# Scale and shift of the first norm: a VectorE product and a GpSimd sum replaced by sixteen ScalarE activations per chunk

## The reference

```python
emb = jax.nn.silu(_sin_emb(timestep)) @ W_ada + b_ada
scale, shift = jnp.split(emb[:, None, :], 2, axis=-1)
x = _ln(src) * (1.0 + scale) + shift
q = (x @ Wq + bq)...            # k and v likewise, from the same x
...
x = x + (ctx @ Wo + bo)
```

## Time and profile before

| | before |
|---|---|
| median of 3 runs | 761.92 us (759.7 to 762.53) |
| profiled execution | 761.58 us, of which the span from first to last instruction is 759.8 us |
| mean granted TensorE clock | 0.857 |
| TensorE matmul busy | 577.8 us (76% of the span) |
| VectorE busy | 481.5 us (63%) |
| ScalarE busy | 262.7 us (35%) |
| GpSimd busy | 281.6 us (37%) |

### The profile page before, as it was taken

The page is one execution under the profiler, slowest core; times in us unless marked ns, Lnnn a source line. Parts: engine busy times, 40 slices in busy tenths (PEclk is TensorE's granted clock), DMA queues, the critical chain, the costliest instruction groups (busy, mean ns, idle before and its releaser), DMA issues.

```text
span 759.8 us, 16208 instructions
## 1 busy us (share of the span) xinstructions
PE 577.8 (76%) x5068; PEld 433.1 (57%) x5069; DVE 481.5 (63%) x1306; ACT 262.7 (35%) x548; POOL 281.6 (37%) x200
## 2 busy tenths in 40 slices
PE   3528678995969978589384871439999999999992
PEld 1415375583754747438383361327777787777771
DVE  5674784899679996717966127714656565655661
ACT  1215534524344153243231401004444444444440
POOL 0831628077055480564705010300423333323332
PEclk9558599998888999779785795559999999999997
DMA  8622474133064321553205673256223222222220
GB/s 291 234 78 66 145 251 141 34 112 110 2 227 190 102 82 40 177 239 112 102 9 166 230 278 137 97 192 227 44 40 47 44 42 42 44 41 36 49 42 1
DMA packets 41144, 86.28 MB, mean 114 GB/s; under 512 B 7317, under 2 KB 31790, under 8 KB 37006
## 3 DMA queue, kind: packets, MB, share of 16 engines
q1 hardware_dynamic: 22896, 65.13, 24.5%
q0 software_dynamic: 7200, 8.60, 6.6%
q10 hardware_dynamic: 11006, 12.01, 5.3%
HBM read 57.18 MB, written 29.44 MB: 114 GB/s over the span
## 4 chain that ended last, share of the span: by engine, by line
PE 55%; DVE 21%; DMA 8%; issue 5%; ACT 3%; POOL 3%; ACTq 3%; POOLq 0%; SPq 0%; DVEq 0%
PE bank L1563 8%; PE bank L1732 7%; PE bank L1554 6%; PE bank L1721 4%; PE bank L1723 4%; PE bank L1722 4%; DMA out_x<-x_kept,ids 4%; DMA stage<-in_moe_w 4%; PE bank L1733 3%; PE bank L1451 2%; PE bank L1518 2%; PE bank L1534 2%; PE bank L1508 2%; DVE split L914 2%; PE bank L1490 2%
## 5 line engine op out<-in xcount | busy, mean ns | idle before, releaser
L1721 PE MATMUL bank<-xs_f,w_moe 128*128 128x128 f16 x624 | 124.1, 221 | 6.9 <-issue 5.5
L1723 PE MATMUL bank<-xs_f,w_moe 128*128 128x128 f16 x624 | 124.1, 221 | 0.0
L1722 PE MATMUL bank<-xs_f,w_moe 128*128 128x128 f16 x624 | 123.6, 221 | 0.0
L825 ACT ACTIVATE stage<-bank,cols 128x128 f32<-128x128 f32 x312 | 88.5, 377 | 95.9 <-PE bank L1723 83.2
L629 POOL DMA_INDIRECT out_x<-x_kept,ids x39 | 61.9, 1587 | 65.0 <-DVE x_kept L1371 34.9
L1721 PEld LDWEIGHTS bank<-xs_f,w_moe 128*128 x624 | 61.4, 98 | 43.1 <-issue 14.1
L1732 PE MATMUL bank<-w_moe,split 128*128 x208 | 78.7, 380 | 0.7
L573 POOL DMA_INDIRECT dispatched<-disp,slot x32 | 34.1, 1067 | 121.0 <-DVE disp L1160 56.7
L1554 PE MATMUL bank<-w_moe 128*128 128x512 f32 x128 | 63.1, 656 | 16.2 <-ACT w_moe L707 16.2
L1416 PE MATMUL bank<-mats,w_moe 128*128 128x128 f32 x96 | 19.9, 375 | 57.2 <-DVE w_moe L957 57.2
L1722 PEld LDWEIGHTS bank<-xs_f,w_moe 128*128 x624 | 61.6, 99 | 2.6
(11 more groups left out here) (242 smaller groups left out, 1275.2 us busy)
## 6 DMA issues: line engine op xcount, KB each, us to landing
stage<-in_moe_w SPq DMA_DIRECT2D x16, 1024.0 KB, 7.8
w_split<-split SPq DMA_DIRECT2D x16, 1024.0 KB, 5.0
w_moe<-w_split SPq DMA_DIRECT2D x8, 2048.0 KB, 8.2
w_moe<-in_bias SPq DMA_DIRECT2D x8, 1024.0 KB, 11.0
xs<-dispatched ACTq DMA_DIRECT2D x41, 130.0 KB, 2.1
w_moe<-in_x_f SPq DMA_DIRECT2D x4, 512.0 KB, 5.6
w_moe<-in_x_t SPq DMA_DIRECT2D x4, 512.0 KB, 5.1
out_x<-x4b ACTq DMA_DIRECT2D x4, 512.0 KB, 5.4
```

Of the source, the lines that this page charges most:

```text
L825: ins = act.activation(h32[j][:, f, :], bank[2 * j + g][:, P * (f % 4):P * (f % 4) + P], ACT.Relu, bias=moe_b1[:, bass.ds(e, 1), f], scale ...
L1721: pe.matmul(o, hi, xs_f[j][:, k, :], start=(k == 0), stop=False)
L1722: pe.matmul(o, hi, xs_f[j][:, KD + k, :], start=False, stop=False)
L1723: mm = pe.matmul(o, lo, xs_f[j][:, k, :], start=False, stop=(k == KD - 1))
```

## The change

The product on VectorE and the sum on GpSimd are removed. ScalarE does both in one: for each feature half k and each of the 8 sequences b, one activation over 64 columns reads PSUM, multiplies with the scale and adds the shift of that sequence (both are one number per partition), and writes `x1`. That makes 16 activations per chunk. In ScalarE's order they stand: for chunk 0 ahead of `split_high(0, 0)`; for chunk 1 between `context(0, 1)` and `split_high(0, 3)`; for chunks 2 and 3 behind the feed-forward activations and ahead of `split_high(c + 1, 0)` and the exponentials.

```diff
-            def shift_norm(c):
-                for k in range(KD):
-                    pool.wait_ge(ada_scaled.sem, ada_scaled.of(c, k + 1))
-                    pool.tensor_tensor(
...
-                        ALU.add).then_inc(x1_ready.sem, 1)
...
             mask(0)
-            pool.wait_ge(cond_ready, 1)
-            shift_norm(0)
             select(1)
             less_maximum(0, 0)
             less_maximum(0, 1)
             probabilities(0, 0)
             probabilities(0, 1)
-            shift_norm(1)
             pool.wait_ge(main_in, N_MAIN)
             select(2)
             for c in range(NCH - 1):
...
                 less_maximum(c + 1, 0)
-                if c + 2 < NCH:
-                    shift_norm(c + 2)
                 less_maximum(c + 1, 1)
...
+            def scale_shift(c):
+                act.wait_ge(v_done.sem, v_done.of(c, 0))
+                act.wait_ge(kept_ready.sem, kept_ready.of(c, 0))
+                for k in range(KD):
+                    act.wait_ge(turn1_done.sem, turn1_done.of(c, k + 1))
+                    for b in range(CB):
+                        at = c * CB + b
+                        ins = act.activation(x1[:, k, S * b:S * b + S], bank[TURN1_BANK[c] + k][:, S * b:S * b + S],
+                                             ACT.Identity, bias=ada[:, KD + k, at:at + 1], scale=ada[:, k, at:at + 1])
+                    ins.then_inc(x1_ready.sem, 1)
...
+            act.wait_ge(cond_ready, 1)
+            scale_shift(0)
             act.wait_ge(main_in, N_MAIN)
             split_high(0, 0)
...
             context(0, 1)
+            scale_shift(1)
             split_high(0, 3)
...
                 feed_forward(c, range(KF))
+                if c + 2 < NCH:
+                    scale_shift(c + 2)
                 split_high(c + 1, 0)
                 exponentials(c + 1, 0)
...
-                def scale_norm():
...
-                        dve.tensor_tensor(x1[:, k, :].rearrange("p (b s) -> p b s", s=S),
...
-                                          ALU.mult).then_inc(ada_scaled.sem, 1)
...
             norms()
-            scale_norm()
             dve.wait_ge(main_in, N_MAIN)
...
             residual()
-            scale_norm, *_ = attention(1)
-            scale_norm()
             split_low(0, 3)
...
                 scores(0)
-                if c + 2 < NCH:
-                    scale_norm, *_ = attention(c + 2)
-                    scale_norm()
                 split_low(c + 1, 0)
```

More of the change, by code:

```diff
@@ L318, in build @@
         xn1_ready, turn1_done = count("xn1_ready", 1), count("turn1_done", 2)
-        ada_scaled, x1_ready = count("ada_scaled", 2), count("x1_ready", 2)
+        x1_ready = count("x1_ready", 2)
         q_done, q_ready = count("q_done", 2), count("q_ready", 2)
@@ L520, in mask @@
                             ALU.add).then_inc(bias_masked[u].sem, 1)
-            def shift_norm(c):
-                for k in range(KD):
-                    pool.wait_ge(ada_scaled.sem, ada_scaled.of(c, k + 1))
-                    pool.tensor_tensor(
-                        x1[:, k, :].rearrange("p (b s) -> p b s", s=S),
-                        x1[:, k, :].rearrange("p (b s) -> p b s", s=S),
-                        ada[:, KD + k, bass.ds(c * CB, CB)].unsqueeze(2).broadcast_to([P, CB, S]),
-                        ALU.add).then_inc(x1_ready.sem, 1)
             def less_maximum(c, u):
@@ L1000, in attention @@
                 vec, finish = stepper(attention_step, c)
-                def scale_norm():
[L1004 to L1007, removed]
-                        dve.tensor_tensor(x1[:, k, :].rearrange("p (b s) -> p b s", s=S),
-                                          bank[TURN1_BANK[c] + k][:].rearrange("p (b s) -> p b s", s=S),
-                                          ada[:, k, bass.ds(c * CB, CB)].unsqueeze(2).broadcast_to([P, CB, S]),
-                                          ALU.mult).then_inc(ada_scaled.sem, 1)
                 def values():
@@ L1037, in sums @@
                         finish()
-                return scale_norm, values, scores, sums
+                return values, scores, sums
             def second_half(c):
@@ L1181, in _ @@
             hidden, residual, norms = adapter(0)
-            scale_norm, values, scores, sums = attention(0)
+            values, scores, sums = attention(0)
             step(dve.tensor_copy(time_f[:], time_i[:]))
@@ L1269, in _ @@
             for c in range(NCH - 1):
-                _, values, scores, sums = attention(c + 1)
+                values, scores, sums = attention(c + 1)
                 (_, _, rotate, norm3, style, choose, token_gates, find_place, copy_gates, accumulate,
```

## The result

The changed kernel takes 763.98 us (median; 762.05 to 765.56), the kernel before 761.34 us on the same chips (759.44 to 762.64). The ratio is 1.0037, with a 95% interval of 1.0027 to 1.0047: it is slower by 2.1 to 3.6 us, 0.37%. The profiled execution is 764.33 us with a span of 762.5 us, against 761.58 and 759.8.

A forecast was written before the change was run, and what follows sets the result against it. The chain through TensorE (55% of the span) and VectorE (21%) was taken as the bound. 2.55 + 0.2 + 0.45 = +3.2 us on the profiled 761.58 gave 764.8; the median's 0.34 made 765.1 us, range 761.5 to 768.5.

The forecast's parts named there:

- The activations: ScalarE's sixteen 64-column activations per chunk: 0.404 us for one, 0.304 us from one to the next, 4.96 us in all.
- Rival (a): ScalarE's activations run slower than worked out, step 0.33 us or more: 766.5 us, up to 769.7; chance 0.25.
- The step itself: First norm, TensorE's transposes to queries: 0 in chunk 0; in chunk 1 queries at 116.19 against 116.09.
- The first selection: GpSimd's selection for chunk 1 moves forward into chunk 0's norm and stalls three VectorE operations: +2.55 us.
- Rival (b): The moved selections don't stall VectorE; chunk 0 costs 0 and chunk 1 0.1: 762.5 us; chance 0.15.
- The second selection: GpSimd's selection for chunk 2 moves into chunk 1's norm; 2.4 us of cover, 0.1 to 0.15 us comes through.
- The cover behind chunk 1's norm: VectorE's 9.49 us idle ahead of 131.29 covers split_low(0, 3) and norm2 ending some 3.5 us later: cost 0.
- Turn c = 0: Loop, chunk 2: split_low ends later, so GpSimd's probabilities start and VectorE's rotation step ends 0.45 us later: +0.45 us.
- Turn c = 1: Loop, chunk 3: the same sequence, but the part split ends before less_maximum lets VectorE in: cost 0.
- (c): Loop, chunk 2: VectorE's rotation slips in ahead of GpSimd's probabilities and wins up to 1.9 us; chance 0.07.
- (d): ScalarE reloads its table for the new activations, 1.3 us, twice in the loop, hitting waiting time; chance 0.01.

The follow-up runs named there:

- the two with shared norm: On the kernel with both repairs, ScalarE does the first feature half and VectorE the second, in chunks 0 and 1 (753.29 us) or chunk 1 alone (754.89 us).
- the filler: The kernel before, with 32 unread transposes on TensorE between chunk 1's transposes and its queries: 761.21 us, ratio 0.9996.
- the moved rotation: The kernel before, with the rotation's odd half ahead of the first half's probabilities on GpSimd: 758.19 us against 762.15, ratio 0.9958.

## Why the prediction was right

The sign, the size and both places were right: 765.1 us forecast, 763.98 measured. By its steps:

- **The activations.** Forecast 4.96 us, measured 4.83 or 4.84 in the three chunks shown. Both terms were off and partly cancel: one takes 439 ns and not 404, and the step from one to the next is (4.84 - 0.44) / 15 = 0.293 us and not 0.304. The first error lies in the price of a column. The two lengths that the prediction names, 1.91 us at 2048 columns and 775 ns at 512, give 0.74 ns and not 0.83, and with 0.74 ns the 775 ns come down to 444 ns at 64 columns. The second is the overlap, 0.439 - 0.293 = 0.146 us, where the rows at 512 columns gave 0.10. So a total within 0.12 us is partly luck. Rival (a), whose step was 0.33 us or more, is out. By the Trainium skill, "ScalarE: Activation LUTs", section "What ACT_TABLE_LOAD costs", one would take 0.425 us and, with an overlap of 93 ns, the sixteen 5.4 us, both estimates. The trace agrees on the one and not on the overlap, and so not on the sixteen.
- **The step itself.** Forecast 0 and, by the shorter transposes of chunk 1, +0.1 us; measured -0.1 us in both chunks, since the sixteen are 0.12 us shorter than worked out.
- **The first selection.** Forecast +2.55 us from a collision that stood elsewhere in the trace; measured +2.54. The edit that holds the selections takes the loss away, and the edit that moves them alone brings all of it. Rival (b) is out. (The +2.54 is this pair of traces; over all thirteen it is 2.3 to 2.8 us.)
- **The second selection.** Forecast +0.1 us through the cover of 2.4 us; nothing came through. The norm ends at 112.56 + 1.38 = 113.94, and TensorE transposes at 114.47 with no idle time ahead. Holding this selection alone gave no gain that can be told.
- **The cover behind chunk 1's norm.** Forecast as cost 0 with 9.49 us idle on VectorE. The idle time ahead of the same operation (now L970) is 6.29 us: 3.2 us of it went, where 3.5 were forecast:

```profile
135.43 0.68 DVE L970 TENSOR_TENSOR w_moe<-bank,add_o 64x512 f32<-64x512 f32 x1 [6.29 <-PE bank L1416]
```

- **Turn c = 0.** Forecast +0.45 us, measured 20.67 - 20.19 = +0.48 us, and L1061 longer by 0.50 us.
- **Turn c = 1.** Forecast 0, and this step failed. L1061 grew by 0.80 us. It takes two things together. The part split now stands at 261.18 for 3.00 us, because ScalarE's part comes late and `less_maximum` runs until 262.04; and TensorE came 1.2 us sooner to the rotation (L1061 starts 18.89 instead of 20.10 us behind the transposes), since its granted clock in this stretch was 1.00 where it had been 0.92 (its eight transposes took 1.06 instead of 1.80 us). Either alone leaves the rotation at 3.28 us: the late split in the two kernels that hold the second selection and keep the changed kernel's order on ScalarE, the early TensorE in the two with shared norm. The prediction took TensorE's pace there from the trace of before, where it was slower. The net is -0.4 us (37.27 instead of 37.69 us from transposes to transposes), which is why the miss does not show in the time.
- **Rivals (c) and (d).** Neither came true: L1061 didn't slip in ahead of the probabilities in any turn, and both traces have 18 table loads.

The steps as measured give -0.2 + 2.54 + 0.48 - 0.4 = +2.4 us; the runs give +2.6. This agreement is closer than the traces support. Between them also lie 1.03 us at the start, 0.5 us between chunk 0's transposes and chunk 1's (62.44 instead of 61.92), and -1.84 us at the end of the first part (48.63 instead of 50.47 us from chunk 3's second-norm to its third-norm transposes), where the feed-forward product of the last chunk took 15.60 instead of 17.08 us at a granted clock of 0.90 instead of 0.82. None of the three comes from the change as far as the other traces show.

What a single trace must not be used for here: from chunk 0's transposes to chunk 1's, the same instructions took 61.92 us in the trace of before and 64.21 and 64.24 us in those of the filler and of the moved rotation, whose edits lie behind this stretch. The views of that stretch for the kernel before and for the moved rotation:

```profile
48.50:110.40 61.90, 46.30 (x437) 0.76 0.46 156
```

```profile
48.50:112.70 64.20, 47.94 (x436) 0.81 0.44 150
```

TensorE is busy for 46.3 us in one and 47.9 in the other, and the higher mean clock stands in the slower one. So a difference of 1 to 2 us at one landmark of one trace says nothing here; what counted above for the selection and for turn c = 0 were differences that come back in every trace with the same cause.

## What to carry to other kernels

When an instruction leaves a list that is executed in order, everything behind it moves forward: ask of each one what it will now stand beside. Here the edited step was even, and an untouched selection, 15 us earlier than it used to be, made the loss. One fused instruction instead of two saves nothing if it must be cut into sixteen with a fixed cost each, while the old pair overlapped over two halves; the same fusion shared by two engines, at the places where TensorE waits, won 1%.

## What the hardware showed that I had not expected

- A wait that is 2.3 us shorter gave nearly twice its length, 3.95 us by the feed-forward behind it: with 2.31 us of idle time ahead, sixteen products of 512 columns took 7.13 us with the granted clock at 1.00 (2.4 GHz throughout), with 4.57 us 8.82 us, the first of them at 0.50 (1.2 GHz; mean of the stretch 0.93).
- Filling the wait with unread transposes gave the same 7.13 us, and no gain for the whole kernel that could be told (0.998 to 1.0011).
- VectorE's multiply and add with one number per partition took 2.11 us for eight 64-column pieces out of PSUM, 0.26 us each, a little less than ScalarE's 2.48.
- A stall behind GpSimd does not vanish when the order is changed: the rotation fell from 3.3 to 0.7 us, and the split behind it rose from 2.23 to 4.24.
